# Cross-attention and ternary feed-forward on one core: from pairs of batches with 64-row tiles to periods of four batches with 32-row tiles

## The reference, cut to what matters

```
xn   = layernorm(x)
q, k, v = xn @ Wq, ctx @ Wk, ctx @ Wv             # 16 heads x 64
dots = q k^T / 8                                  # per head, 64 x 64
dots = where(mask[key], -FLT_MAX, dots)           # the mask drawn is all False
dots = where(key > row, -FLT_MAX, dots)           # causal
x    = x + softmax(dots) v @ Wo + bo
xn   = layernorm(x); xq = round(xn * 127 / max|xn|)   # int8-like, per row
h    = silu(xq @ tern(w_gate)) * (xq @ tern(w_up))
hq   = round(h * 127 / max|h|)
out  = x + hq @ tern(w_down)
```

## Time and profile before

| | us |
|---|---|
| runs, median (3) | 806.67 (806.22 to 807.98) |
| the profiled execution's own time | 807.29 |
| its span (first to last instruction) | 805.3 |
| TensorE busy | 776.1 |
| VectorE busy | 678.5 |
| ScalarE busy | 653.8 |
| GpSimd busy | 407.0 |

### The profile page before, as it was taken

How to read it: one execution, slowest core, us unless ns; L and a number is a source line. 1 busy time by engine, 2 the same in 40 slices (tenths; PEclk the granted TensorE clock), 3 DMA queues, 4 the chain that set the end, 5 groups by cost and what they waited for, 6 DMA issues and landing times.

```text
span 805.3 us, 15033 instructions
## 1 busy us (share of the span) xinstructions
PE 776.1 (96%) x5294; PEld 527.6 (66%) x5294; DVE 678.5 (84%) x1844; ACT 653.8 (81%) x1138; POOL 407.0 (51%) x404
## 2 busy tenths in 40 slices
PE   7899999999999999999999999999999999999982
PEld 5667666666766766666676666667667666766551
DVE  7749888888988888888888888888888889887984
ACT  4688888888888888888888888888888888888770
POOL 1235546455454555555555555555554555545551
PEclk9999999999999999999999999999999999999996
DMA  8100010211111020111102011120210211011011
GB/s 233 50 1 14 21 53 16 59 14 44 30 27 53 12 62 15 30 44 27 53 8 58 22 28 47 27 54 8 53 27 21 54 27 27 8 27 27 14 27 27
DMA packets 71937, 29.19 MB, mean 36 GB/s; under 512 B 36277, under 2 KB 71351, under 8 KB 71863
## 3 DMA queue, kind: packets, MB, share of 16 engines
q1 hardware_dynamic: 71862, 28.24, 13.7%
HBM read 15.64 MB, written 4.19 MB: 25 GB/s over the span
## 4 chain that ended last, share of the span: by engine, by line
PE 89%; DVE 7%; issue 1%; DMA 1%; ACT 1%; POOL 1%; POOLq 0%; DVEq 0%
PE ps_s L431 14%; PE ps_a L492 14%; PE ps_s L402 5%; PE ps_s L322 4%; PE ps_kv L402 4%; PE ps_kv L322 4%; PE ps_s L403 3%; PE ps_s L324 3%; PE ps_s L404 3%; PE ps_kv L323 3%; PE ps_s L323 3%; PE ps_kv L403 3%; PE ps_kv L324 3%; PE ps_kv L404 3%; PE ps_a L453 3%; PE ps_b L453 3%
## 5 line engine op out<-in xcount | busy, mean ns | idle before, releaser
L859 POOL TENSOR_TENSOR prob<-prob,row_max 128x1024 f32<-128x1024 f32 x64 | 121.9, 1905 | 178.7 <-DVE row_max L734 178.7
L512 ACT ACTIVATE vp<-ps_s 64x512 f32<-64x512 f32 x256 | 151.2, 591 | 34.0 <-PE ps_s L404 28.8
L877 POOL TENSOR_TENSOR prob<-prob,row_rec 128x512 f32<-128x512 f32 x128 | 130.7, 1042 | 56.5 <-DVE row_rec L809 56.5
L512 ACT ACTIVATE vp<-ps_kv 64x512 f32<-64x512 f32 x256 | 151.4, 591 | 7.6
L869 POOL TENSOR_TENSOR hid_b<-hid_q,neg_round 128x512 bf16<-128x512 f32 x64 | 66.5, 1040 | 120.4 <-DVE hid_q L778 120.4
L492 PE MATMUL ps_a<-vp,prob_t 128*64 128x128 f32 x2048 | 125.9, 276 | 0.9 <-DVE x L756 0.6
L431 PE MATMUL ps_s<-kp,xn_t 128*64 128x512 f32 x512 | 124.0, 605 | 2.8 <-ACT vp L512 1.8
L492 PEld LDWEIGHTS ps_a<-vp,prob_t 128*64 128x64 f32 x2048 | 110.6, 137 | 24.2 <-issue 16.4
L731 DVE TENSOR_TENSOR prob<-ps_s,bias_sb 128x1024 f32<-128x1024 f32 x64 | 78.3, 1224 | 51.0 <-PE ps_s L431 51.0
L836 POOL TENSOR_TENSOR rs<-ve,neg_half 128x1 f32<-128x1 f32 x128 | 70.2, 548 | 36.5 <-DVE ve L656 24.0
L512 ACT ACTIVATE kp<-ps_s 128x512 f32<-128x512 f32 x130 | 77.7, 598 | 11.9 <-PE ps_s L290 8.1
(11 more groups left out here) (171 smaller groups left out, 1670.3 us busy)
## 6 DMA issues: line engine op xcount, KB each, us to landing
x_in<-in_x SPq DMA_DIRECT2D x16, 256.0 KB, 3.2
ctx_in<-in_ctx SPq DMA_DIRECT2D x16, 256.0 KB, 3.4
x_res<-in_x SPq DMA_DIRECT2D x16, 256.0 KB, 3.1
out<-x SPq DMA_DIRECT2D x15, 256.0 KB, 2.3
hid_t<-hid_b SPq DMA_TRANSPOSE x64, 2.5
kp<-in_L_xattn_Wk SPq DMA_DIRECT2D x1, 512.0 KB, 3.7
kp<-in_L_xattn_Wq SPq DMA_DIRECT2D x1, 512.0 KB, 4.6
kp<-in_L_xattn_Wv SPq DMA_DIRECT2D x1, 512.0 KB, 5.5
```

The source lines that it names most:

```text
L512: copy = lambda dst, src, **kw: nc.scalar.activation(dst, src, ACT.Copy, **kw)
L859: p.tensor_tensor(prob[c % 2][:], prob[c % 2][:], rows(row_max[c % 2]), ALU.subtract).then_inc(shifted, 1)
L877: p.tensor_tensor(prob[c % 2][:, heads, :], prob[c % 2][:, heads, :], rows(row_rec[c % 2])[:, heads, :], ALU.mult).then_inc(normed, 1)
```

## The change: what it does, and the diff

- A step becomes a **period** of four batches (32 of them). Its 256 rows are two 128-row tiles: tile 2n holds rows 32 to 63 of the four batches ("up"), tile 2n+1 rows 0 to 31 ("low"). Low rows get 32 keys only, so low scores are 16 heads x 32 keys = one bank.
- Scores and attention products use four 32-column tiles side by side, one per batch, and stand in one stretch: `scores(n)`, then `attend(n-1)`.
- V' is copied out of PSUM whole (128 partitions) to `v_rows`, and 24 DMAs a period bring it to the partitions that the products need (`move_v`): `vp` for the up rows, `vq` (four heads x 32 keys) for the low rows. ScalarE's 64-partition copies go.
- Rows whose keys are all masked need the mean of V' over keys 32 to 63 too: `late_sum`, `late_rep`, `n_sum`, one matmul `late` and `add_late` a period.
- The rounding of the hidden block moves from VectorE to ScalarE (`round_hid`); small VectorE and GpSimd operations take both tiles at once.
- x, x_res and out move one tile per DMA (64 KB, `tile_rows`), and LN1 of the second group moves out of the setup. Feed-forward lags by one period (gate/up) and two (down).

```diff
+    def tile_rows(t, k):
+        n, first_row = k // 2, R if k % 2 == 0 else 0
+        return t[QB * n:QB * n + QB, first_row:first_row + R, :]
...
+            def move_v(n, i):
+                c, h2 = i // 2, i % 2
+                sp.wait_ge(v_evac, V_UNITS * n + 2 * i + 2)
+                for b in range(2):
+                    sp.dma_start(vp[c][h2 * S:(h2 + 1) * S, b, :, :],
+                                 v_rows[i][b * S:(b + 1) * S, :, :]).then_inc(vp_moved[i], 16)
+                for a2 in range(2):
+                    h4 = 2 * a2 + h2
+                    for b in range(2):
+                        sp.dma_start(vq[c][h4 * R:(h4 + 1) * R, b, :, :],
+                                     v_rows[i][b * S:b * S + R, QB * a2:QB * a2 + QB, :]).then_inc(vq_moved[i], 16)
...
+            for n in PERIODS:
+                g, r = n // 2, n % 2
+                if live(n, 2):
+                    for c in range(2):
+                        sp.wait_ge(hb_ready, 2 * (n - 2) + c + 1)
...
+                        sp.dma_start_transpose(hid_t[:, c, :, :], hid_b[:, c, :]).then_inc(ht_moved, 16)
+                if makes_k(n) and r == 1:
+                    sp.wait_ge(x1_done, 2 * g)
+                    load_x(x_res[(g + 1) % 2], g + 1, xres_loaded[(g + 1) % 2])
+                if live(n):
+                    if n:
+                        sp.wait_ge(attn_ready, n)
+                    for i in range(4):
+                        move_v(n, i)
+                if live(n) and r == 1 and g + 3 < GROUPS:
                     load_inputs(g + 3)
+                if live(n, 2):
+                    for c in range(2):
+                        store(2 * (n - 2) + c)
...
+            def scores(n):
...
+                for half in range(2):
...
+                    for r in range(QB):
+                        rows = slice(2 * r0 * P + r * R, 2 * r0 * P + r * R + R)
+                        key = (r0 * QB + r) * S
+                        t = mm(ps_up[r * R:(r + 1) * R, half * BANK:(half + 1) * BANK], xn_t[par][:, rows],
+                               kp[par][:, half * 8:half * 8 + 8, key:key + S], start=True, stop=True)
...
+                for r in range(QB):
...
+                    t = mm(ps_low[r * R:(r + 1) * R, :], xn_t[par][:, rows],
+                           kp[par][:, :, key:key + R], start=True, stop=True)
...
+            def attend(n):
+                pe.wait_ge(pt_evac, 3 * n + 3)
+                for i in range(4):
+                    pe.wait_ge(vp_moved[i], 32 * n + 32)
+                    pe.wait_ge(vq_moved[i], 64 * n + 64)
...
+                for a in range(HP):
+                    for r in range(QB):
+                        t = mm(ps_a[r * R:(r + 1) * R, 0:D], prob_t[:, a, r * R:(r + 1) * R], vp[r // 2][:, r % 2, 4 * (a % 2) + a // 2, :],
+                               start=(a == 0), stop=(a == HP - 1))
+                for a in range(QB):
+                    for r in range(QB):
+                        t = mm(ps_a[r * R:(r + 1) * R, D:2 * D], prob_t[:, HP + a, r * R:(r + 1) * R],
+                               vq[r // 2][:, r % 2, a, :], start=(a == 0), stop=(a == QB - 1))
```

More of the change, by code:

```diff
@@ L203, in build, with ln1_pairs @@
+        fills = lambda n: 0 if not live(n) else V_UNITS + (K_UNITS if makes_k(n) else 0)
+        def ln1_pairs(n):
+            return [m for m in ([2, 3] if n == 0 else [n + 3]) if live(n) and 2 * m < TILES]
+        PERIODS = range(QUADS + 2)
         block = es.enter_context(nc.Block())
@@ L265, in _ @@
+            for i in range(2):
+                sp.wait_ge(stored[i], 16 * GP * (GROUPS // 2))
         @block.tensor
@@ L281, in transpose_ctx, with transpose_x @@
                 t.then_inc(ctxt_ready, 1)
+            def transpose_x(par, dst):
+                for k in range(GP):
+                    t = nc.tensor.transpose(dst[:, k * P:(k + 1) * P], xn[par][:, k, :], id_sb[:])
+                t.then_inc(xnt_ready, 1)
             def transpose_weights(w):
@@ L311, in _ @@
                     t.then_inc(m_ready, 1)
-            def transpose_x(par):
-                for k in range(GP):
-                    t = nc.tensor.transpose(ps_a[:, k * P:(k + 1) * P], xn[par][:, k, :], id_sb[:])
-                t.then_inc(xnt_ready, 1)
             def k_unit(h, par, dst):
@@ new lines, in _ @@
+            for n in PERIODS:
+                if live(n):
+                    scores(n)
+                if n == 0:
+                    rest_of_setup()
+                if live(n, 1):
+                    attend(n - 1)
+                fill(n, 0)
+                fill(n, 1)
+                turn(n)
+                fill(n, 2)
+                fill(n, 3)
+                if live(n):
+                    late(n)
+                if live(n, 2):
+                    down(n - 2)
+                fill(n, 4)
+                if live(n, 1):
+                    transpose_xq(n - 1)
+                fill(n, 5)
+                fill(n, 6)
+                if live(n, 1):
+                    gate_up(n - 1, 0)
+                fill(n, 7)
+                fill(n, 8)
+                fill(n, 9)
+                if live(n):
+                    prob_transposes(n, 0)
+                fill(n, 10)
+                if live(n, 1):
+                    gate_up(n - 1, 1)
+                if live(n):
+                    prob_transposes(n, 1)
+                fill(n, 11)
+                fill(n, 12)
+                if live(n):
+                    prob_transposes(n, 2)
+                fill(n, 13)
+                fill(n, 14)
+                fill(n, 15)
@@ L880, in _ @@
-            slots(slot, 3)
+                        p.tensor_tensor(prob_up[:, heads, :], prob_up[:, heads, :],
+                                        rows(row_rec[:, 0, heads], 8, S), ALU.mult).then_inc(normed, 1)
+                    p.tensor_tensor(prob_low[:], prob_low[:], rows(row_rec[:, 1, :], H, R), ALU.mult).then_inc(normed, 1)
+                for m in ln1_pairs(n)[1:]:
+                    rstd1(m)
+                if n % 2 == 1 and makes_k(n):
+                    residual(g + 1)
+                    spread_late(g + 1)
```

987 lines of the change are left out of this document (520 added, 467 removed).

## The result

The changed kernel takes 901.14 us (median of four runs, 897.00 to 904.38) where the kernel before takes 806.47 on the same chip: 1.117 times, interval 1.112 to 1.122. It is 95 us slower, and the forecast was 740. The profiled execution spans 902.6 us.

A forecast was written before the change was run, and what follows sets the result against it. TensorE bounds the kernel: a period of 23.54 us loses 2.15 and 0.44, gains 0.3, giving 21.25, with stalls 21.4. 805.3 - 30 x 2.14 - 7 = 734, plus 5 is 739: 740 us, range 722 to 808.

The forecast's parts named there:

- the whole stretch 5.4 as taken: TensorE's scores and attention products together, four tiles overlapping: 5.4 us a period in place of 7.54.
- rival 2: TensorE issues at 30 ns an instruction: scores and products take 7.1 us, period 23.1, kernel about 793; chance 0.10.
- the two-at-a-time case: Only two TensorE tiles overlap in scores and products: stretch 10.3 us, kernel 892 us; chance 0.05.
- near 500: Sign to look for in the profile: ScalarE's busy time near 500 us.
- near 560: Sign to look for in the profile: VectorE's busy time near 560 us.
- Rival 1: VectorE's chain is longer than walked: one us more a period, kernel 771 us; chance 0.12.
- V' by DMA: SyncE's 24 moves a period, 3.15 MB, taken as hidden in 9 us at 350 GB/s: cost 0.
- rival 3: V' moves become the bound, passing 21.4 us below 215 GB/s and 23.54 below 188; chance 0.11 slower, 0.07 partly late.
- 15.6 to 19.8 of 21.4 us: SyncE's queue per period: moves 10.3 to 13.7 us, two transposes 2.4, tile DMAs and ctx load 2.9 to 3.7.
- with several us of room: SyncE's stores and next hidden block's transposes, queued behind the V' waits, were said to have several us to spare.
- My loop over `attend` and the moves: V' cycle: 2.1 us + transfer + 2 landing + 2.7 attention; passes 21.4 us at a transfer of 14.6.
- Each us of lateness is one us a period: Price if V' moves land after `attend` wants them: one us a period per us late.

The follow-up runs named there:

- experiment 8: Experiment 3's twelve moves and bytes, but each move over all 128 partitions, values misplaced; 742.4 us.
- experiment 9: Changed kernel with its 24 V' moves carrying only an eighth or a quarter of their bytes; 818.1 us.
- experiments 2 to 5: Changed kernel with 2: half bytes, 821.3 us; 3: twelve moves, 983.8; 4: eight moves on ScalarE's queue, 877.3; 5: as 3, destination halves alternating, 944.3.
- experiment 3: Changed kernel with the same V' bytes in 12 DMAs a period in place of 24, still 64 and 32 partitions each; 983.8 us.
- the padded one: Changed kernel without vq: low rows' probabilities zero-padded to 64 keys to use vp, 8 moves a period in place of 24; 770.1 us.
- experiment 12: Changed kernel with V' sent through a buffer in HBM, 16 DMAs a period over 128 and 64 partitions; 2648 us.

## Why the prediction was wrong

**What held.** Without the moves the kernel takes 735.3 us against 740, and its period is 21.0 against 21.4. That the time is so near is partly luck: 0.4 us over 31 periods are 12 us less than forecast, so setup and ends cost some 8 us more than the sum had for them. Four 32-column tiles overlap fully: in the rows of experiment 8 the scores span 2.8 us and the products 2.8 (6 rounds of 0.43 and 24 of 0.107 were 2.56 and 2.57), the whole stretch 5.4 as taken. The issue limit of 30 ns (rival 2) and the two-at-a-time case are out. ScalarE's 498 us and VectorE's 571 are within 2% of "near 500" and "near 560". Rival 1 is out too: with wide moves the period is 21.1 us, so VectorE's chain does not stretch it.

**What failed** is one line, **V' by DMA, "Cost taken: 0"**. It rested on a rate, on a sum of the queue's issues, and on a price for being late; none of the three held.

- *The rate.* "At 350 GB/s with the DMA engines full 3.15 MB are 9 us: hidden." That row is of loads from HBM into all 128 partitions. Half-wide moves inside SBUF fill the engines at about 200 GB/s: 16 us. The text had this as rival 3, with the thresholds 215 and 188 GB/s, and gave it 0.11; it is a part of what happened. What I set against it was one number from a transfer of another shape. The text's own sentence, "no row shows SBUF to SBUF", should have kept that row from deciding.
- *The issues.* I took 0.43 to 0.57 us from the earlier trace rows and walked the queue against when `attend` wants V', 24.1: last landing at 19.9 or 24.3, thus late by 0.2 already at the upper end. The whole queue I summed to "15.6 to 19.8 of 21.4 us", and of what stands behind the moves I wrote "with several us of room". Measured where bytes play no part, in experiment 9, an issue with the gap behind it is 0.63 and the list of a period 23.1 us: more than TensorE's 21.0, before a byte is counted. The low terms were the issue (0.61 with no gap for 0.43 to 0.57), the transpose (1.6 in the mean for 1.19) and the gaps, for which the sum had nothing. The period is 23.3 there, 2.3 more than without moves: 71 of the 83 us of experiment 9. My loop over `attend` and the moves does not give them: with 15.1 us in place of its edge of 14.6 it passes 21.4 by 0.5 us, 16 us in all. I had summed the queue but not held it, as a loop of its own, against the period.
- *The products.* The loop had 2.7 us for them. They took 5.3 in the round above, where the granted clock reads 0.52 at 402 to 406 us (1.2 of 2.4 GHz is 0.5), 0.62 behind, and 1.00 again from 410 on. One contraction has a median of 421 ns over all of the changed kernel and a shortest of 269:

```profile
L478 PE MATMUL ps_a<-vp,prob_t x2048: 269/421/423, 62.6 to 877.4; 128*32 128x128 f32 x187
```

It is not so in every round. Of the 29 that start between 116 and 848 us, 24 took 4.1 to 5.4 us and 5 took 2.8, at full clock. The length of the stall doesn't sort them: behind 3.43 us of waiting at 116.38 they took 5.3 at a granted clock of 0.50, behind 3.47 us at 195.93 they took 2.8 at 1.00:

```profile
195.93 1.96 PE L478 MATMUL ps_a<-vp,prob_t 128*32 128x128 f32 x64 [3.47 <-DMA vq<-v_rows]
197.67 1.08 PE L482 MATMUL ps_a<-vq,prob_t 128*32 128x128 f32 x32
```

What decides between them stays open. In the mean of all 31 waits a round waits 3.9 us (120.8 / 31), and it has 4.4 us of products for 2.8; less the 0.5 us a period that TensorE idles without the moves (14.15 us of 600) that is 5.0, the difference of the periods, 26.0 and 21.0. "Each us of lateness is one us a period" was too low for it: 1.6 of the 5.0 us are the slower products.

**How the 166 us divide.** The runs give a two by two, over the 735.3 of no moves: number alone (24 small) 83; number and full width (24 wide) 99; number and half width (the change) 166; twelve wide 7; twelve half-wide 248 (with a later start of the first group, which was not tried by itself). Width without fewer moves leaves 99, fewer moves without width cost more still, both together 7. The first two are the full queue, 586 of 600 us in both. The changed kernel has both at once: its queue issues for 536 us, with 35 of small gaps and 30 of waiting, and behind the full DMA engines a `vq` issue takes 0.71 us in the mean where it took 0.61. That is why experiments 2 to 5, each easing one of the two, could not bring the gain back.

The Trainium skill (SBUF — State Buffer, Door 1: The DMA port swizzle), which the prediction weighed, gives 8 of 16 ports for 64 partitions in one half, as an estimate 218 GB/s. The runs agree: about 200 (179 to 236) for the half-wide moves of experiment 3, 288 to 388 for the wide ones of 8; that it is the ports, no run shows by itself. It was the one source that spoke of the shape in question, and I left it out of the chances.

**What stays open.** Whether a version exists that puts V' in the right partitions with wide moves only; the 742 us of experiment 8 is what twelve such moves cost, and the best complete kernel here is the padded one, 770 us. Whether it is the reading or the writing side of a move that must be wide was not tried. Nor was a kernel that leaves the 24 moves alone and takes the loads of x and ctx, the stores and the transposes off SyncE's queue, about 7 us of its 23.1; at 200 GB/s its moves would still take some 16 us, over the 14.6 us where rival 3 begins.

## What to carry to other kernels

A transfer's rate may be taken from a row only if that row has its width: count the partitions that one DMA touches on each side, and where a shape has no row, let the bound decide and not the nearest large number. Sum every issue of a queue over a period, transposes and gaps too, and hold the sum against the period as a bound of its own, since issues of one queue stand one behind the other at 0.6 us each even with the DMA engines 30% busy. And put the moves into the loop that closes over buffer release, copy, move and use. And a little more arithmetic (a third more transposes of probabilities and product matmuls) that saved 16 small moves a period was worth 131 us.

## What the hardware showed that was not expected

- Moves within SBUF of 64 or 32 partitions fill the DMA engines at about 200 GB/s (experiment 3: 179 to 236), and crossing from one half of the partitions to the other costs nothing on top (978 against 984 us). Over all 128 partitions they reach 288 to 388 (experiment 8).
- SyncE's queue can be the bound with the DMA engines 30% busy: 24 moves of 16 and 32 KB and 8.5 other DMAs a period kept it issuing, small gaps included, for 586 of 600 us (experiment 9).
- A second issuing queue for 8 of the 24 moves gave back 24 us of 166.
- Behind the stalls 64 product matmul records took up to 3.64 us, at a granted clock of 0.5, where they take 1.93 to 1.96 at full clock. Stalls of the same 3.4 to 3.5 us were followed by the one or by the other.
- Loads whose source has an outermost count of 2 ran at 51 GB/s with a DMA share of 0.13 (experiment 12).
